# The last 64 rows of the down products of two tiles, on the two halves of the array's rows

## What is computed

```
def fp4_linear(x, w):
    return einsum('bsk,nk->bsn', fp4_quant_dequant(x), fp4_quant_dequant(w))
h = silu(fp4_linear(x, w_gate)) * fp4_linear(x, w_up)      # 256 -> 704
y = fp4_linear(h, w_down)                                  # 704 -> 256
x = x + 0.5 * y                                            # x layer-normed on the way in
```

## Time and profile before

| | us |
|---|---|
| median of 3 runs | 3248.5 (3247.22 to 3249.37) |
| the profiled execution: its time | 3248.44 |
| its span | 3246.6 |
| PE busy | 2717.0 (84%) |
| DVE busy | 2650.3 (82%) |
| POOL busy | 2175.2 (67%) |
| ACT busy | 1705.8 (53%) |

### The profile page before, as it was taken

One profiled execution on the slowest core, in us unless ns is written; L12 is line 12 of the kernel. 1 busy time (PEld: TensorE's weight loads), 2 busy tenths in 40 slices (PEclk: granted clock), 3 DMA queues, 4 the chain that ended last, 5 costly groups with the idle time before them and its releaser, 6 DMA issues. The chain is left out here.

```text
span 3246.6 us, 31734 instructions
## 1 busy us (share of the span) xinstructions
PE 2717.0 (84%) x10349; PEld 1394.6 (43%) x10349; DVE 2650.3 (82%) x2498; ACT 1705.8 (53%) x2427; POOL 2175.2 (67%) x1219
## 2 busy tenths in 40 slices
PE   2999999776878878978978978878867659999998
PEld 1565556452324424424414424424422125655555
DVE  6777777407999999999999999999999946777775
ACT  3444444335665756666666666666654513444443
POOL 4566666306787877877777787777787735555652
PEclk9999999987888978979978978978966669999999
DMA  3011111108678687686776776767767720110100
GB/s 103 20 49 40 49 49 39 43 13 195 155 174 198 158 194 179 163 199 167 175 189 172 179 191 165 187 167 176 189 164 187 188 75 14 33 33 26 32 26 20
DMA packets 173304, 387.82 MB, mean 119 GB/s; under 512 B 22502, under 2 KB 90150, under 8 KB 172902
## 3 DMA queue, kind: packets, MB, share of 16 engines
q1 hardware_dynamic: 155382, 367.06, 45.5%
q10 hardware_dynamic: 17776, 18.94, 2.0%
HBM read 308.26 MB, written 52.49 MB: 111 GB/s over the span
## 5 line engine op out<-in xcount | busy, mean ns | idle before, releaser
L971 POOL TENSOR_TENSOR mix_scan<-mix_scan,mix_bc 128x1024 f32<-128x1024 f32 x512 | 1204.6, 2355 | 396.0 <-DVE mix_scan L1126 395.3
L1126 DVE TENSOR_TENSOR_SCAN mix_scan<-mix_decay,mix_ps_du 128x1024 f32<-128x1024 f32 x512 | 1170.0, 2285 | 63.1 <-ACT mix_decay L1072 20.6
L1138 DVE TENSOR_TENSOR mix_ps_du<-mix_ps_du,mix_bc 128x1024 f32<-128x1024 f32 x512 | 618.2, 1207 | 134.6 <-PE mix_ps_du L1239 134.0
L1239 PE MATMUL mix_ps_du<-mix_stack,mix_sel 96*128 96x512 bf16 x1024 | 366.6, 446 | 376.5 <-DVE mix_scan L1126 355.0
L716 PE MATMUL ffn_ps_gate_up<-ffn_w_gate_up,ffn_xT 128*128 128x512 f32 (+1 forms) x1536 | 656.5, 564 | 14.3 <-DVE ffn_h L480 14.0
L1072 ACT ACTIVATE mix_decay<-mix_decay,mix_a_neg 128x1024 f32<-128x1024 f32 x512 | 573.7, 1141 | 114.2 <-DMA mix_decay<-delta_rows 113.2
L755 PE MATMUL ffn_ps_down<-ffn_w_down,ffn_hT 128*128 128x256 f32 (+1 forms) x1536 | 382.4, 391 | 12.1 <-ACT ffn_hT L639 12.1
L716 PEld LDWEIGHTS ffn_ps_gate_up<-ffn_w_gate_up,ffn_xT 128*128 128x128 f32 x1536 | 273.1, 191 | 259.6 <-issue 218.3
L1239 PEld LDWEIGHTS mix_ps_du<-mix_stack,mix_sel 96*128 96x128 bf16 x1024 | 78.6, 103 | 685.6 <-DVE mix_scan L1126 554.9
L612 POOL TENSOR_TENSOR ffn_h_scaled<-ffn_h,ffn_h_recip 128x1408 f32<-128x1408 f32 x64 | 188.3, 2943 | 235.4 <-ACT ffn_h_recip L689 235.4
L1221 PE MATMUL mix_ps_y<-mix_scan,mix_red 128*32 128x512 f32 x2048 | 340.3, 747 | 4.8 <-POOL mix_scan L971 4.8
(11 more groups left out here) (136 smaller groups left out, 3712.8 us busy)
## 6 DMA issues: line engine op xcount, KB each, us to landing
mix_decay<-delta_rows SPq DMA_DIRECT2D x512, 512.0 KB, 7.1
mix_stack<-mix_parts SPq DMA_DIRECT2D x384, 64.0 KB, 2.0
delta_rows<-mix_delta SPq DMA_DIRECT2D x32, 512.0 KB, 3.1
ffn_x<-_attn_hidden_states_dram SPq DMA_DIRECT2D x32, 256.0 KB, 3.1
after_ffn<-ffn_y SPq DMA_DIRECT2D x32, 256.0 KB, 3.2
normed_ffn<-ffn_y_normed SPq DMA_DIRECT2D x32, 256.0 KB, 3.2
mix_x_tokens<-normed_ffn SPq DMA_DIRECT2D x32, 256.0 KB, 12.1
mix_x_residual<-after_ffn ACTq DMA_DIRECT2D x32, 256.0 KB, 4.0
```

The costliest lines, as they stand in the source:

```text
L971: G.tensor_tensor(wt, wt, bc[:, r % 2, 1, :], ALU.mult).then_inc(hc_done, 1)
L1126: V.tensor_tensor_scan(w[:, slot % RING, :], da[:, slot % SPREADS, :], ps_du[:, slot % 2, :], 0.0, ALU.mult, ALU.add).then_inc(scan_done, 1)
L1138: V.tensor_tensor(ps_du[:, slot % 2, :], ps_du[:, slot % 2, :], bc[:, r % 2, 0, :], ALU.mult)\
L1239: ins = M(ps_du[:, slot % 2, h * 512:(h + 1) * 512], const.sel[0:SEL, i, :], stack[:, c % 2, q, h * 512:(h + 1) * 512], start=True, stop=True)
```

## The change

Between the two tiles of a pair, `hq` is laid out anew: the 640 first columns of tile 0, those of tile 1, then the last 64 of tile 0 and the last 64 of tile 1 side by side. `turn_h(0)` now has 5 transposes; `turn_h(1)` has its own 5 and a sixth over the 128 shared columns, which puts tile 0's last rows on partitions 0 to 63 and tile 1's on 64 to 127. `down(0)` leaves its sum open after five products; `down(1)` ends with two products over 64 rows, the first on partitions 0 to 63 into tile 0's sum, the second on 64 to 127 into tile 1's. The last block of `w_down` stands twice in its tile, once on each half, for which the preparation has an additional copy at two of its transposes. The two sums and `turn_x(0)` have a PSUM tensor each (the program's allocator gives each PSUM tensor whole banks, so these are three banks). `keep_h` is one ACT instruction for each tile, `hq` two POOL instructions. `result(0)` stands behind the block scales, ahead of `result(1)`. The store of `w_down` and its load are one DMA each instead of two.

```diff
@@ prepare, ACT
-            nc.scalar.activation(dst, pst[0:cols, n % 2, 0:rows], ACT.Copy).then_inc(kept, 1)
+            ins = nc.scalar.activation(dst, pst[0:cols, n % 2, 0:rows], ACT.Copy)
+            if cols == LASTK:
+                lastcol = (n - len(turns) + ND * KD) // KD * P
+                ins = nc.scalar.activation(wd[LASTK:2 * LASTK, KD - 1, lastcol:lastcol + P],
+                                           pst[0:cols, n % 2, 0:rows], ACT.Copy)
+            ins.then_inc(kept, 1)
-        act.dma_start(wd_out[:, 0:KD - 1, :], wd[:, 0:KD - 1, :]).then_inc(stored, 16)
-        act.dma_start(wd_out[0:LASTK, KD - 1, :], wd[0:LASTK, KD - 1, :]).then_inc(stored, 16)
+        act.dma_start(wd_out, wd[:, :, :]).then_inc(stored, 16)
@@ ffn
-    psDX = a.ps("down", [P, 2, D])
-    psH, psD = psT[:, 0:KH * P], psDX[:, 0, :]
-    psX = [psDX[:, 1, :], psT[:, KH * P:KH * P + D]]
+    psD = [a.ps(f"down{t}", [P, D]) for t in range(2)]
+    psX0 = a.ps("x_turned", [P, D])
+    psH = psT[:, 0:KH * P]
+    psX = [psX0[:, :], psT[:, KH * P:KH * P + D]]
+    REST = (KH - 1) * P
@@ ffn, SP
-            sp.dma_start(wd[:, 0:KH - 1, :], wd_in[:, 0:KH - 1, :]).then_inc(sig.w_loaded, 16)
-            sp.dma_start(wd[0:LASTK, KH - 1, :], wd_in[0:LASTK, KH - 1, :]).then_inc(sig.w_loaded, 16)
+            sp.dma_start(wd[:, :, :], wd_in).then_inc(sig.w_loaded, 16)
@@ ffn, DVE
-            if Y:
-                result(0, j, i)
             if L:
...
             if Y:
+                result(0, j, i)
                 result(1, j, i)
@@ ffn, POOL
-                G.tensor_tensor(blocks(hq[:, l2, :]), blocks(hn[:, l2, :]), spread(hs[:, (j - 1) % 4, :]),
-                                ALU.mult).then_inc(sig.hq_done, 1)
+                of = hn[:, l2, :].rearrange("p (t n b) -> p t n b", t=2, b=QBLOCK)
+                by = hs[:, (j - 1) % 4, :].rearrange("p (t n) -> p t n", t=2).unsqueeze(3)\
+                    .to_broadcast([P, 2, NH, QBLOCK])
+                for lo, hi in ((0, REST // QBLOCK), (REST // QBLOCK, NH)):
+                    to = hq[:, l2, 2 * lo * QBLOCK:2 * hi * QBLOCK]
+                    ins = G.tensor_tensor(to.rearrange("p (t n b) -> p t n b", t=2, b=QBLOCK), of[:, :, lo:hi, :],
+                                          by[:, :, lo:hi, :], ALU.mult)
+                ins.then_inc(sig.hq_done, 1)
@@ ffn, ACT
-            A.activation(hT[:, t, 0:(KH - 1) * P], psH[:, 0:(KH - 1) * P], ACT.Copy)
-            A.activation(hT[0:LASTK, t, (KH - 1) * P:KH * P],
-                         psH[0:LASTK, (KH - 1) * P:KH * P], ACT.Copy).then_inc(sig.hT_kept, 1)
+            hi = REST + t * P
+            A.activation(hT[:, t, 0:hi], psH[:, 0:hi], ACT.Copy).then_inc(sig.hT_kept, 1)
@@ ffn, PE: turn_h
-            for k in range(KH):
-                c = min(P, F - k * P)
-                ins = nc.tensor.transpose(psH[0:c, k * P:(k + 1) * P],
-                                          hq[:, j % 2, t * F + k * P:t * F + k * P + c], ident[:, :])
+            for k in range(KH - 1):
+                ins = nc.tensor.transpose(psH[:, k * P:(k + 1) * P],
+                                          hq[:, j % 2, t * REST + k * P:t * REST + (k + 1) * P], ident[:, :])
+            if t == 1:
+                ins = nc.tensor.transpose(psH[:, REST:], hq[:, j % 2, 2 * REST:], ident[:, :])
@@ ffn, PE: turn_x
-                if on(j, i, -2):
-                    pe.wait_ge(sig.y_done, i * 2 - 3)
@@ ffn, PE: down
-            if on(j, i, -3) or (t == 1 and on(j, i, -2)):
-                pe.wait_ge(sig.y_done, i * 2 + (t - 4))
-            if t == 1 and on(j, i, 1):
-                pe.wait_ge(sig.xT_kept, i * 2 + 3)
-            for k in range(KH):
-                c = min(P, F - k * P)
-                ins = M(psD, hT[0:c, t, k * P:(k + 1) * P], wd[0:c, k, :],
-                        start=(k == 0), stop=(k == KH - 1))
-            ins.then_inc(sig.down_done, 1)
+            if on(j, i, -3):
+                pe.wait_ge(sig.y_done, i * 2 + (t - 5))
+            for k in range(KH - 1):
+                M(psD[t][:, :], hT[:, t, k * P:(k + 1) * P], wd[:, k, :], start=(k == 0), stop=False)
+            if t == 1:
+
+                for half in range(2):
+                    rows = slice(half * LASTK, (half + 1) * LASTK)
+                    M(psD[half][:, :], hT[rows, 1, REST:], wd[rows, KH - 1, :], start=False, stop=True)\
+                     .then_inc(sig.down_done, 1)
```

## The result

The changed kernel takes **3308.1 us** (3306.65 to 3311.61, four runs) and the kernel before, beside it, 3247.97 (3247.22 to 3249.37, four runs). The ratio is 1.0186, with a 95% interval of 1.0169 to 1.0204: slower by 1.9%, where I had forecast 1.7% faster. The profiled execution of the changed kernel spans 3304.7 us.

A forecast was written before the change was run, and what follows sets the result against it. PE bounds the feed-forward stages; each step saves 0.81 + 0.11 - 0.01 + 0.05 = 0.96 us, so 55.7 + 1.4 - 0.4 + 0.4 = 57.1 us off 3248.4 gives 3191.3, called 3192; range 3187 to 3199.

The forecast's parts named there:

- the second margin: On ACT: keep_h(0), behind the square that the moved result(0) delays by 0.33 us, still starts in time, with 0.02 left.
- the two pieces of slack on ACT: Ahead of PE's wait for keep_h(0): 0.02 us of margin, and 0.16 more from tile 0's copy losing its second part.
- The bound: Feed-forward steady part: PE always busy, steps of about 17.1 us, so PE savings count in full, 0.96 us a step.
- The visit: End of down(1): two 64-row products run side by side for 0.01 us more, next gate-and-up group 0.62 after first start.
- in order by passes: 64-row visit: only one of four passes overlaps, 0.216 us more a visit, 12.5 us dearer, 3204; chance 0.12.
- no sharing: 64-row visit: the two halves' products run one after the other, 25 us dearer, 3217; chance 0.08.
- The copy: keep_h(1) on ACT: one copy of 768 columns takes 0.81 us instead of 0.86, gaining 0.05 a step.
- the slower rival: POOL's split hq, reading h_scaled with a stride, takes three times as long: 68 us slower, 3317; chance of slower 0.04.
- The margins: Two waits of PE stay just hidden: gate_up(1)'s weight load after gated(0) by 0.05 us, keep_h(0) by 0.02.
- the margins break: h_done or keep_h(0) comes 0.1 to 0.3 us late each step, giving back 6 to 18 us, 3198 to 3210; chance 0.07.
- The sum: Whole kernel: 55.7 us from 2 x 29 steps of 0.96, plus 1.4, -0.4 and +0.4, in all 57.1 us faster.

The follow-up runs named there:

- e3: Kernel before, with an unused 0.37 us bn_stats on DVE ahead of result(1), moving x_scaled by 0.33 us: 3366.64 us, ratio 1.0355.
- e8: e1 with the old transposes, copies and hq, both 64-row products on rows 0 to 63 of the array: 3221.3 us, ratio 0.9921.
- e1: Changed kernel with x_scaled ahead of both result instead of behind them: 3186.89 us, ratio 0.981 to the kernel before.
- e2: Changed kernel, DVE's order untouched, with POOL's h_scaled waiting for x_scaled of the same step: 3186.93 us, ratio 0.9811 to the kernel before.
- e9: Changed kernel with h_scaled cut into four POOL instructions of 352 columns: 3206.43 us, ratio 0.9871 to the kernel before.
- e4: Kernel before, with one memset of 64 columns on DVE ahead of result(1), moving x_scaled by 0.07 us: 3252.14 us, ratio 1.0007.
- e5: e1 without tile 1's product over the last 64 rows: 3190.73 us, ratio 0.9825 to the kernel before.

## Why the prediction was wrong

**The step that failed** is the second margin: "`result(0)` has moved ... Where it stands now it delays `x_scaled`, and so ACT's square, which ran from 2864.96 to 2865.59 and now ends at 2865.92 ... Margin 0.02". It moves the start of `x_scaled` by 0.33 and takes its duration of 0.68 as fixed. The shift was right: 0.19 ahead became 0.14 behind. The duration became 3.00, and the square, at 2864.96 plus 0.33 in the forecast, came 2.3 later than that. The sum asked for every moved instruction who waits for it, and never what runs beside it at its new place.

What the trace of before had to say on this, and I didn't read: POOL's `h_scaled` takes 2.93 in a full step, but 2.60 at the head of a stage, where `x_scaled` doesn't meet it. In the timeline of the first stage of before:

```profile
88.64 2.60 POOL L612 TENSOR_TENSOR ffn_h_scaled<-ffn_h,ffn_h_recip 128x1408 f32<-128x1408 f32 x1 [7.08 <-ACT ffn_h_recip L689]
```

The same POOL work with two durations, a third of a microsecond apart, and a two-input DVE instruction that starts within 0.2 of it: that was the row to follow. It harmed nobody before, since POOL has slack.

The Trainium skill, SBUF — State Buffer, "Who interferes with whom", has this rule: a DVE instruction with two inputs in SBUF contends with a GpSimd (POOL) instruction that reads SBUF, because they share a pair of ports that is an exclusive lock. Of DVE's 2-port modes it says that whoever issues first has the pair for the whole instruction while the other blocks, and in general: "Issue order, not op shape, decides who blocks." The trace agrees for two inputs in SBUF as well, with 3.00 against 0.68 on one side and 2.93 against 2.59 on the other, and with 1.20 where POOL's instruction was in four. That the ports are the reason is the Trainium skill's word; the runs show only the exclusion and its order.

**The size.** The page's mean of 2648 ns mixes two kinds. In each stage `x_scaled` ran ahead of `h_scaled` in the first 4 of its 32 instructions, with 0.63 to 0.69, and was held in the other 28, with 2.85 in the first stage and 3.00 in the second: 56 of 64. In the middle of a stage a step lost 18.29 - 16.19 = 2.10, near its ends 18.22 - 16.19 = 2.03, so 56 give 114 to 118 us. The measured difference between the changed kernel and that with the sums last is 121.2. In four places of the two stages (near 234, 2865, 2995 and 3016 us) the granted clock also falls to the 1.2 GHz level for a while after the wait; one of them here, in the windows and in PE's timeline of the changed kernel:

```profile
2860.00:2880.00 20.00, 18.02 (x64) 11.14 (x63) 14.77 (x21) 6.78 (x13) 9.48 (x7) 0.91 0.09 27
```

```profile
2864.88 4.11 PE L760 MATMUL ffn_ps_down<-ffn_w_down,ffn_hT 128*128 128x256 f32 x10 [1.98 <-ACT ffn_hT L649]
```

After the wait of 1.98, `down(0)` takes 4.11 instead of the 2.42 of other steps, 1.7 more. Four times that is 7, and the sum 121 to 125. The wait alone doesn't bring this about: e3 has a wait of 1.82 in front of `down(0)` too, and its granted clock is 1.00 throughout both stages (130 to 640 and 2740 to 3300 us). What else it takes isn't shown. The 2.10 of a step is about the 3.00 less 0.68, 2.32, less the two pieces of slack on ACT that the prediction named, 0.02 and 0.16.

**Point by point.**
- *The bound* was right for as long as PE waits for nothing: a step takes 16.19 against 17.19 in the middle of a stage and 17.12 near its ends, 1.00 and 0.93 less, where I had 0.96.
- *The visit* was right: 0.63, the second product free, as taken from the mixer's groups of four. (The "two records of 0.43" of one such matmul alone were read from the gate-and-up rows, of as many columns; no row shows one alone.) The second and the third rival (in order by passes, no sharing) are out: the visit would have taken 0.84 or 1.06, and took the latter only in the kernel that keeps to one half of the rows.
  The Trainium skill, TensorE: Matmul & The Clock Gate, Part 3, "The mechanism", says both that row groups run at once and that matmuls start in program order; the trace agrees with the first. The second, record by record with one product's two ahead of the other's, would make 0.84, the rival's figure. The trace has the four starts at 0, 0.01, 0.32 and 0.33, and the two records that raise the semaphore, the last of each product, are the second pair; in e8 the starts are product by product. Whether the records of the changed kernel are issued in another order isn't shown.
- *The copy* of 768 columns took 0.81, as forecast. The split `hq` took 2.73 together where I had 2.59 + 0.2, so the slower rival that I named, a strided POOL, is out too.
- *The margins* of 0.05 and 0.02 both held in e1 and e2, where the order is right again: PE is busy there for all of the 69 us of either stretch. The rival "the margins break" had the right place (idle time before L760, put down to `ffn_hT`) but a price of 0.1 to 0.3 where it was 1.84: it thought of a late start, not of a long instruction.
- *The sum* of 57.1 us came out as 61.4 (3248.3 to 3186.9) once the exclusion was out of the way. That it is near is in part luck. From the fifth to the last `x_scaled` of each stage, 54 steps in all, it is 926.9 us before and 876.1 in e2: 50.8 less, 0.94 a step, where I had 0.96. The other 10.6 us of the medians lie in the first and last steps of the stages, the preparation and the mixer, where I had 5.3 (four more steps and 1.4 for the ends). What brought the rest there I didn't trace.
- *The chances*: 0.04 for slower was held by one mechanism on POOL's side, that of a slow instruction. A mechanism between two engines that both touch the same memory wasn't among the cases.

## What to carry to other kernels

Before a DVE instruction with two inputs in SBUF is moved, even by 0.3 us, look at what POOL starts and runs at its old and its new place: the order of the two starts was worth 2.3 us here beside a POOL instruction of 2.59, and it turned a gain of 1.9% into a loss of 1.9%. A POOL or DVE instruction with two durations for the same shape in one trace, as POOL's 2.60 and 2.93 here, is a sign that it may happen already. If the order matters, fix it, by place or by a wait on the engine that has slack, rather than leave it to a lead of 0.04 to 0.19 us.

## What the runs showed of the hardware

- The exclusion lasts for one instruction of the holder, and the held one's record runs on from its own start: `x_scaled` ended 0.55 after POOL's `h_scaled`, or after its first piece in e9, where it was behind.
- It isn't the record's start that decides to the last digit. DVE won when its record began up to 0.035 after POOL's (e4) and lost at 0.053 (e3) and more; what happens between a record's start and the moment that decides, the runs don't show.
- Small POOL instructions are held like long ones. One over 128x2, count, shortest, median and longest ns, first and last start in the changed kernel:

```profile
L604 POOL TENSOR_TENSOR ffn_shift<-ffn_shift,ffn_minus_one x64: 196/1581/1584, 55.6 to 3205.2; 128x2 f32<-128x2 f32 x64
```

  In the step shown it starts at 2909.11, 0.10 after a rounding of `h` on DVE (two inputs in SBUF, 1.62 long), takes 1.58 and ends 0.06 after it; in the first steps of a stage it takes 0.20. It lies in POOL's slack here.
- DVE instructions with one input in PSUM and one in SBUF neither held POOL nor were held. In the changed kernel `h_scaled` started while the two `result` (a sum in PSUM and a tile of `x`) were running and took its 2.59, and `gated(1)` (2912.01) started 1.2 into POOL's `hq` and took 0.89, as `gated(0)` does in the earlier trace rows without it.
- Two fp32 products over 64 rows each, on different halves of the array and into different PSUM tensors, take the time of one, both records of each and the weight loads included: 0.63 to the next matmul in the changed kernel and in e5. In the changed kernel each of them raises a semaphore.
